# A low-rank correction folded into the FFN weight, and PV matmuls issued behind the scores of odd steps

## The reference

```python
h = layernorm(x)
q, k, v = split(h @ Wqkv + bqkv)                # 16 heads of 64
a = softmax(causal(q @ k.T * 64**-0.5)) @ v
x = x + a @ Wproj + bproj
h = layernorm(x)
x = x + (h @ W.T + b) + (h @ V_r) @ C.T         # V_r, C: [1024, 32]
```

## Time and profile before

| | us |
|---|---|
| median of two runs (846.64 and 849.77) | 848.21 |
| the profiled execution | 850.17 |
| its span, on core 5, the slowest | 848.5 |
| spans of all cores | 836.7 to 848.5 |
| TensorE busy (matmul) | 656.5 |
| ScalarE busy | 331.2 |
| VectorE busy | 288.9 |
| GpSimd busy | 185.5 |

### The profile page before, as it was taken

One profiled execution on the slowest core, in us unless ns is written; L12 is line 12 of the kernel. 1 busy time (PEld: TensorE's weight loads), 2 busy tenths in 40 slices (PEclk: granted clock), 3 DMA queues, 4 the chain that ended last, 5 costly groups with the idle time before them and its releaser, 6 DMA issues.

```text
span 848.5 us, 10484 instructions; the slowest of 8 cores (836.7 to 848.5 us)
## 1 busy us (share of the span) xinstructions
PE 656.5 (77%) x3433; PEld 280.7 (33%) x3433; DVE 288.9 (34%) x717; ACT 331.2 (39%) x449; POOL 185.5 (22%) x304
## 2 busy tenths in 40 slices
PE   0399999999147778788697977978888898965666
PEld 0144444444032323333233333333333333322222
DVE  2543534301023433425324333232313232244342
ACT  0131413232004365645446465656575757500000
POOL 2000000000105533515322222222222222113211
PEclk9999999999655578888989979899889898968898
DMA  8991200000752000000100001010101010102001
GB/s 169 216 209 37 74 27 25 0 1 1 126 97 76 0 1 1 26 25 26 49 26 26 27 24 51 1 50 1 51 1 51 1 49 2 51 25 73 27 25 50
DMA packets 15125, 38.13 MB, mean 45 GB/s; under 512 B 3401, under 2 KB 3425, under 8 KB 15073
## 3 DMA queue, kind: packets, MB, share of 16 engines
q0 software_dynamic: 7616, 11.67, 8.8%
q1 hardware_dynamic: 7457, 25.79, 8.8%
HBM read 39.68 MB, written 8.39 MB: 57 GB/s over the span
## 4 chain that ended last, share of the span: by engine, by line
PE 62%; DVE 13%; issue 8%; ACT 7%; POOL 5%; DMA 4%; DVEq 0%; SPq 0%; ACTq 0%; POOLq 0%
PE ps_sc L251 13%; PE ps_pv L403 12%; PE ps_sc L422 7%; PE ps_pv L276 7%; PE ps_w L549 5%; PE ps_w L626 4%; PE ps_bf L235 4%; PE ps_pv L626 4%; DVE wq_a L488 3%; ACT xf_a L431 3%; POOL xf_a L442 3%; DMA xf_a<-wffn 3%; ACT xnt_a L431 3%; PE ps_sc L549 2%; POOL xnt_a L442 2%
## 5 line engine op out<-in xcount | busy, mean ns | idle before, releaser
L431 ACT ACTIVATE xf_a<-ps_sc 128x1024 bf16<-128x1024 f32 (+1 forms) x192 | 166.2, 893 | 131.8 <-PE ps_sc L422 130.6
L422 PE MATMUL ps_sc<-q_fm,k_fm 64*128 64x512 bf16 (+3 forms) x640 | 121.6, 404 | 55.9 <-ACT xf_a L431 31.3
L431 ACT ACTIVATE xnt_a<-ps_sc 128x1024 bf16<-128x1024 f32 (+3 forms) x128 | 111.8, 898 | 121.2 <-PE ps_sc L422 120.6
L403 PE MATMUL ps_pv<-xf_a,v_on 128*66 128x512 bf16 (+3 forms) x384 | 113.7, 396 | 8.9 <-POOL xf_a L442 5.1
L251 PE MATMUL ps_sc<-xnt_a,wq_a 128*128 128x512 bf16 x512 | 115.7, 385 | 0.9 <-DVE xnt_a L317 0.9
L442 POOL TENSOR_TENSOR xf_a<-xf_a,tri_sb 128x128 bf16<-128x128 bf16 x152 | 60.5, 425 | 195.1 <-ACT xf_a L431 194.9
L422 PEld LDWEIGHTS ps_sc<-q_fm,k_fm 64*128 64x128 bf16 x640 | 30.8, 96 | 156.1 <-issue 153.8
L442 POOL TENSOR_TENSOR xnt_a<-xnt_a,tri_sb 128x128 bf16<-128x128 bf16 x104 | 42.1, 430 | 177.7 <-ACT xnt_a L431 177.6
L403 PE MATMUL ps_pv<-xnt_a,v_on 128*66 128x512 bf16 (+3 forms) x256 | 75.5, 388 | 4.9 <-POOL xnt_a L442 2.5
L251 PEld LDWEIGHTS ps_sc<-xnt_a,wq_a 128*128 128x128 bf16 x512 | 50.2, 99 | 60.4 <-issue 4.5
L210 ACT ACTIVATE ln_t<-mv,eps_t 128x1 f32<-128x1 f32 x32 | 9.3, 290 | 142.8 <-DVE mv L205 142.8
(11 more groups left out here) (65 smaller groups left out, 590.0 us busy)
## 6 DMA issues: line engine op xcount, KB each, us to landing
xf_a<-x SPq DMA_DIRECT2D x32, 512.0 KB, 3.9
y<-xf_a SPq DMA_DIRECT2D x16, 512.0 KB, 2.7
wq_a<-wqkv POOLq DMA_DIRECT2D x3, 2048.0 KB, 38.8
wq_a<-wproj POOLq DMA_DIRECT2D x1, 2048.0 KB, 19.3
xf_a<-wffn POOLq DMA_DIRECT2D x4, 512.0 KB, 25.7
bias_a<-bqkv POOLq DMA_DIRECT2D x1, 512.0 KB, 55.7
bias_a<-bffn POOLq DMA_DIRECT2D x1, 512.0 KB, 59.3
bias_a<-bproj SPq DMA_DIRECT2D x1, 512.0 KB, 5.9
```

Source lines behind the costliest of these rows:

```text
L403: e.matmul(ps_pv[hd][0:66, off * 128:512], v_on[:, ki2, 66 * hh:66 * hh + 66], chunkpair(cp)[:, hd * 512:hd * 512 + ncol], start=st, stop=sp),
L422: e.matmul(ps_sc[:, pp * 1024 + hd * 512 + off * 128: pp * 1024 + hd * 512 + 512], k_fm[hp:hp + 64, hc, ki * 128:(ki + 1) * 128], q_fm[hp: ...
L431: e.activation(chunkpair(cp).rearrange("p (a n) -> p a n", a=2) [:, :, 0:ncol], ps_sc[:, pp * 1024:(pp + 1) * 1024] .rearrange("p (a n) -> ...
```

## The change

Three edits.

1. V_r is transposed too (eight transposes and a copy into `vrT`), and V_r C^T is added to the FFN weight in place: for each of eight row blocks and two halves one matmul of 32 rows and 512 columns, alternately into `ps_w` and `ps_pv[0]`, and one add on VectorE. All of it stands ahead of the first head pair.
2. `gen_C2` loses the eight matmuls of u, their copy, and the matmul with `ct_bf` in each half. The `yield` behind them stays.
3. `pop_pv()` on odd steps is called after the scores, the exp and the masks of that step, ahead of `pump()`.

```diff
         r_psbf = m_ct
+        vrT = xnt_a[0:32, 7168:8192]
+        for c in range(KC):
+            m_trv = P.op("pe", lambda e, c=c: e.transpose(
+                             ps_bf[0:32, c * 128:(c + 1) * 128], vr_bf[:, c, :], id_b[:]), ...)
+        m_vrT = P.op("dve", lambda e: e.tensor_copy(vrT[:, :], ...), waits=[m_trv], sig="dv")
+        fold_banks = [ps_w[:, 0:512], ps_pv[0][:, 0:512]]
+        fold_r = [m_bqkvT, m_v_evac[0]]
+        for kc in range(KC):
+            for half in range(2):
+                pb = (kc * 2 + half) % 2
+                mmc = P.op("pe", lambda e, kc=kc, half=half, pb=pb:
+                           e.matmul(fold_banks[pb],
+                                    vrT[:, kc * 128:(kc + 1) * 128],
+                                    ct_bf[0:32, half * 512:(half + 1) * 512],
+                                    start=True, stop=True),
+                           waits=[m_vrT, m_ct, fold_r[pb]], sig="pe")
+                m_fold = P.op("dve", lambda e, kc=kc, half=half, pb=pb, mmc=mmc:
+                              e.tensor_tensor(
+                                  wt_bf[:, kc, half * 512:(half + 1) * 512],
+                                  wt_bf[:, kc, half * 512:(half + 1) * 512],
+                                  fold_banks[pb], ALU.add), ...)
+                fold_r[pb] = m_fold
...
-        m_pv_read = [m_v_evac[0], m_v_evac[1]]
+        m_pv_read = [m_pv_read0_fold, m_v_evac[1]]
-        r_psw = m_bqkvT
...
-                if ki % 2 == 1:
-                    pop_pv()
                 pp = gki % 2
...
                 gki += 1
+                if ki % 2 == 1:
+                    pop_pv()
                 pump()
...
-            for kc in range(KC):
-                mmu = P.op("pe", ... e.matmul(ps_w[0:32, 0:128], vr_bf[:, kc, :], hTv[:, i2, kc, :], ...)
-            m_u = P.op("dve", lambda e: e.tensor_copy(u_bf, ps_w[0:32, 0:128]), waits=[mmu], sig="dv")
-            r_psw = m_u
             yield
...
-                w0 = [m_hT, m_wt_evac]
+                w0 = [m_hT, m_wt_final]
...
-                mmf = P.op("pe", lambda e, half=half:
-                           e.matmul(fdst(half), u_bf,
-                                    ct_bf[0:32, half * 512:(half + 1) * 512],
-                                    start=False, stop=True), ...)
```

More of the change, by code:

```diff
@@ L367, in build_nc @@
         r_psbf = m_ct
+        vrT = xnt_a[0:32, 7168:8192]
+        m_trv = None
+        for c in range(KC):
+            m_trv = P.op("pe", lambda e, c=c: e.transpose(
+                             ps_bf[0:32, c * 128:(c + 1) * 128], vr_bf[:, c, :], id_b[:]),
+                         waits=[m_vr, r_psbf] if c == 0 else [],
+                         sig="pe" if c == KC - 1 else None)
+        m_vrT = P.op("dve", lambda e: e.tensor_copy(
+                         vrT[:, :], ps_bf[0:32, :].rearrange("p (c n) -> p c n", c=KC)),
+                     waits=[m_trv], sig="dv")
+        r_psbf = m_vrT
+        fold_banks = [ps_w[:, 0:512], ps_pv[0][:, 0:512]]
+        fold_r = [m_bqkvT, m_v_evac[0]]
+        m_fold = None
+        for kc in range(KC):
[11 more added lines that the diff above has]
+                                  wt_bf[:, kc, half * 512:(half + 1) * 512],
+                                  fold_banks[pb], ALU.add),
+                              waits=[mmc, m_wt_evac if kc == 0 and half == 0 else None],
+                              sig="dv")
+                fold_r[pb] = m_fold
+        m_wt_final = m_fold
+        r_psw = fold_r[0]
+        m_pv_read0_fold = fold_r[1]
         pair_reader = [m_qkv_done, m_qkv_done]
@@ L601, in gen_C2 @@
             hTv = xn_b.rearrange("p a (c n) -> p a c n", c=KC)
-            mmu = None
-            for kc in range(KC):
[L604 to L610, removed]
-            r_psw = m_u
             yield
@@ L624, in gen_C2 @@
                 for kc in range(KC):
-                    P.op("pe", lambda e, half=half, kc=kc, i2=i2:
+                    mmf = P.op("pe", lambda e, half=half, kc=kc, i2=i2:
                          e.matmul(fdst(half),
@@ L628, in gen_C2 @@
                                   wt_bf[:, kc, half * 512:(half + 1) * 512],
-                                  start=(kc == 0), stop=False),
+                                  start=(kc == 0), stop=(kc == KC - 1)),
                          waits=w0 if kc == 0 else [],
-                         sig=None)
+                         sig="pe" if kc == KC - 1 else None)
                     if kc == 3:
                         yield
-                mmf = P.op("pe", lambda e, half=half:
-                           e.matmul(fdst(half), u_bf,
-                                    ct_bf[0:32, half * 512:(half + 1) * 512],
-                                    start=False, stop=True),
-                           waits=[m_u, m_ct] if half == 0 else [],
-                           sig="pe")
                 m_y = P.op("dve", lambda e, i2=i2, half=half, mmf=mmf: e.scalar_tensor_tensor(
```

## The result

| | us, median | runs |
|---|---|---|
| before | 849.17 | 10 |
| after | 842.85 | 11 |

Two of the eleven executions of after (875.9 and 916.0 us) had the cores of one die at a lower clock, and all ratios in this document leave such executions out. The ratio is 0.9929, with a 95% interval of 0.9913 to 0.9946. That is 6.0 us off 849.2: faster, by less than the 2% that a measurement of this kernel tells surely from no change. The forecast was 835 and 825 to 847. The sign and the range held. The gain of 13.8 us did not: less than half of it came.

What follows compares the result with a forecast made beforehand. Bounds: TensorE's wait for the FFN weight, the first group's chain, later pairs partly at 1.2 GHz, and the tail chain. 15.2 - 7.0 - 11.5 - 10.5 = -13.8 from 850.2, less 1: 835 us, range 825 to 847 (own 828 to 842).

Steps and rivals of the forecast that it cites:

- Part 1: Ahead of the first scores: adding V_r C^T to the FFN weight costs 15.2 us, with nothing beside it.
- Part 2: Correction matmuls removed from 16 FFN tiles: -7.0 us in six tail tiles, -11.5 us in ten filler tiles.
- they are worth what they take when fast, about half: FFN tiles: removing the eight V_r matmuls gains 0.45 to 0.5 us per tile, not the 0.83 they hold TensorE.
- Rival C: Tail: second halves of six FFN tiles stay at the slow clock, +10 us, 845 in all; chance 0.07.
- Part 3: PV behind odd steps' scores: 0.65 us in each of 13 light pairs, 0.2 in 11 full ones, together -10.5 us.
- rival A: Light head pairs: the reorder is worth nothing, ScalarE's gap only moves from step 5 to 6; 846 us, chance 0.15.
- Without the slow clock it would be 1.0: Light pair of the second group: reordering PV would gain 1.0 us at full clock instead of some 0.5.
- rival D: Later head pairs: PV fills waits of steps 3 and 4, so the clock stays up; -10 us, 825, chance 0.16.

Runs made afterwards that it cites:

- number 2: The kernel after with PV put back ahead of the scores of odd steps, fold and removal kept; 0.9957 of before.
- number 3: The kernel before with only the correction matmuls left out, no fold, old order, output lacking the correction; 0.9856 of before, -12.2 us.
- number 8: The kernel after without the fold's instructions, the correction left out; 0.9823 of before.
- number 7: The kernel after with the eight V_r matmuls put back in the six tail FFN tiles, result unused; 0.9983 of before, 4.6 us over after.
- number 12: The kernel after with the old PV order and the eight V_r matmuls kept, unused, in the ten filler FFN tiles; 1.0019 of before.
- number 6: The kernel after with V_r C^T computed while TensorE waits for W, and W's transposes added to it; 0.9668 of before, 822.2 us.
- number 11: The kernel of number 6 with PV put back ahead of the scores of odd steps; 0.9721 of before.

## Why the prediction was right in sign and wrong in size

By whole times the account is short. Fold and removal together (number 2) gave -3.7 us for a forecast of 15.2 - 18.5 = -3.3; the order on top gave -2.4 for -10.5. The first agreement is luck: the removal alone gave -12.2 for -18.5, and the fold cost 8.6 to 9.0 for 15.2, and the two misses cancel.

**Part 1, the fold, right for its stretch.** +15.3 for +15.2 in the stretch that it stands in, nothing beside it, and no wait behind it. In the whole time only some 9 us of it show, as the tail is shorter with it (numbers 3 and 8).

**Part 2, the removal, near in sum, with its terms wrong.** -16.1 in the full pairs with their part of the order (forecast -13.5), -6.8 in the tail (forecast -7.0); but alone (number 3) it gave the tail only -2.0. The premise "they are worth what they take when fast, about half" fell: number 7 puts the eight at 0.86 us. The estimate from the Trainium skill ("TensorE: Matmul & The Clock Gate", section "Back-to-back issue gap"), weighed there, gives 0.65. At full speed a row of number 7 shows 0.54 us for eight (start to next start). As a duration the forecast's half was near and the page's figure too high; as a gain both were too low:

```profile
797.37 0.61 PE L638 MATMUL ps_w<-xn_b,vr_bf 128*32 128x128 bf16 x8 [0.94 <-DVE xn_b L627]
797.91 5.31 PE L656 MATMUL ps_pv<-wq_a,xn_b 128*128 128x512 bf16 x16
```

The slow matmuls behind it show the rest: the clock fell within the 16 that follow (5.31 us for 3.61). Rival C, the clock takes back the tail's gain, was true in part: slow time in the tail rose from 35 to 39 us.

**Part 3, the order: the step that failed.** The prediction put 0.65 us on each of 13 light pairs, -8.5. The count was wrong: only seven pairs carry at most transposes, and they gained 1.7 us in sum. So was the price. Exp 5 came earlier, but by 0.53 us in the pair of the earlier trace rows and 1.23 in the late pair shown, where 0.9 and, for its like, 2.1 were reckoned; exp 6 moved by 0.05 and 0.33, and the end of the pair by 0.32 and 0.42, since four PV and ScalarE's gap now stand one step later. That was rival A, "the gap of ScalarE only moves", and it was right in part.

Two pairs on one core, both with a stretch of the low clock in them, could not carry a price for all. "Without the slow clock it would be 1.0" was false in sign: at the full clock there was no gap, and the second and third pair of the second group get 0.3 and 0.7 us longer. Late pairs do gain 0.4 to 0.9 at like clock, about the 0.8 reckoned, but only at 0.91; at 0.83, where 15 of 24 stand in after, at most 0.2.

The sum also lacked a term: what the removal does to the light pairs. Alone it makes them 4.5 us longer (number 3; the seven 0.9) with 18 us more at 1.2 GHz. In its presence the order takes the slow time back (102 to 81 us, 104 to 82.5), and with it 3.7 us of light (the seven 2.7) and 3.0 to 4.0 of full pairs. That is the direction of rival D, the clock stays up, but only against a loss that D did not foresee: the order alone leaves slow time at 90 us, above before's 85, and the clock of groups 1 to 3 ends where it was, 0.90 for 0.89 on core 5. The two add up, for the light pairs by place, to +4.5 - 3.7 = +0.8, the row of the first table. The new order alone, with nothing to repair, was worth 3.8 us. That the clock carries these losses and gains is inferred from slow time and pair lengths moving together; no run set the clock by itself.

The single edits don't add: -3.8 for the order, -12.2 for the removal and +8.6 to +9.0 for the fold by the difference of whole times, +15.3 by its stage. The Trainium skill ("TensorE: Matmul & The Clock Gate", section "What's actually happening") says that activity releases the slow clock. The removal's +18 us agree in direction; number 12, which puts eight of the ten matmuls back into each filler tile and lifts nothing, does not. What distinguishes one pattern of the clock from another stays open; so does why the tail is 5.7 us longer without the fold's instructions (number 8). Only the fold's values and the start of the scores were excluded.

## What to carry to other kernels

Work that must be added goes where the chain already waits: the same fold cost 15 us ahead of the scores, 12 us spread over steps that had free time by the shares (on one bank), and nothing beside a transfer that TensorE waited more than 20 us for. Ask then what holds back the issue of that transfer: here it was the wait of another load ahead of it in the issuing engine's list, and the swap was worth 12 us more (822.2 to 810.3). Judge a reordering at the end of the repeated piece, on all cores and at like clock, not at the instruction that comes early in one of them; and where the granted clock of a stage is between its two levels, run each part alone and together before adding their gains.

## What the runs showed of the hardware

The add of 128x1024 in bf16 with one operand in PSUM took 0.69 us (240.67 in number 6), the same as the plain copy of that shape from PSUM. The Trainium skill ("VectorE: DVE Perf Modes", section "The perf-mode tier table") puts an addition of two tensors with a PSUM operand at the single rate; half of what it gives there for 2048 fp32 elements at that rate, 2293 ns, would be an estimate of 1.15 us. The measurement decides: here it took 0.6 of that, so the additions of number 6 cost no more than the copies that they replace. The fold's add, with an fp32 operand in PSUM, took 0.69 us for half as many elements, 128x512 (265.39 in after).

The place of the low clock moves whole tiles: the same 16 matmuls of 128x512 took between 3.61 us and 6.55 in the tail of after, and tails with the same 281 matmuls took from 98.35 us (number 11) to 106.3 (number 8) in the mean of eight cores.
